# Set-up of a four-layer model: who splits the output weights and copies the first queries

## The chip, the cores and the metric

One core of one Trainium2 chip runs the whole program. The time is the device time of one execution in microseconds.

## The reference

The model adds four layers to x (2 batches, 1024 rows, 256 columns):

```python
x = x + attention0(x)   # layer norm, 16 heads of 64, one shared key/value head, queries and keys
                        # l2-normalised, causal, relative-position bias from a small MLP, null key
x = x + attention1(x)   # layer norm, scaled queries, bias read from memory, null key
x = x + moe2(x)         # 8 experts, two taken per row, and a shared expert
x = x + moe3(x)
# attention0, cut to what matters
sim  = concat([q . null_key, q @ k.T]) * 8 + concat([null_bias, bias])
attn = softmax(where(causal & mask, sim, -big))
out  = ln((attn @ concat([null_value, v])) @ Wout, g_out)
```

The change touches only the set-up for attention0. Weights are used as two float16 halves: high = f16(256 w), low = f16(256 w - high), and a product is three matrix products of halves.

## The kernel before, in words

Five engines (TensorE, VectorE, ScalarE, GpSimd, and SyncE for loads) each run a list written out in program order and meet at semaphores. The attention of both layers is one loop over head-steps n: a step T is a tile of 128 rows (16 steps over two layers), with 8 units u (four groups of four heads, two batches) of 4 heads, so 512 head-steps. The loop begins at n = -20: what stands at n < 0 is the set-up and the lead of the pipeline. With m, k = divmod(n, 4), an engine's work for unit u is written at fixed places: at k = 1 the query product of unit m + 3 (TensorE) and its squares and copy (ScalarE, L862, L864); at k = 2 the reciprocal root and scaling on GpSimd (L611 to L615); at k = 3 the transposes of unit m + 2 (TensorE L1679), the high half `q_b` (ScalarE L853), the low half into the lower partitions of `q_a` (VectorE L1285), and a copy of the high half into the upper partitions of `q_a` (GpSimd, `query_copy`, L558). Scores of head i come at n = i - 3 (L1655, L1656), `biased` and `neg_max` at n = i - 2 on VectorE (L1253), the exponential at i - 1, and transposes, halves (ScalarE L932, VectorE L1351) and the product with v from n = i.

Weights land in `stage` (two buffers). In the set-up ScalarE scales and rounds to the high half (`weight_half`, and `out_half` with two instructions L772 and L775 for each half of the output weights), and GpSimd makes the low half in pieces of 256 columns (`low_half`, L529): 2 pieces of wkv, 8 of wq, 8 of wo. It does the first wq pieces at n = -12 and the other six at n = -9; the wo pieces stand one at the end of each head-step from n = -7 to 0. The semaphore `job_done` counts all pieces; TensorE waits on it before it uses wq and wo, SyncE before it fills a stage buffer again.

The null key enters as 16 extra columns, `w_nk`: VectorE multiplies the rows of Wq with the null key (`null_product`, L1153), sums over each head (L1158) and splits the sums into halves (`null_columns`, L1140, L1141). TensorE multiplies with them at n = -7. The null logits of unit u are then two small GpSimd steps (L653, L654) at k = 3, m = u - 2; the first of unit 0 at n = -5.

The bias of attention0 comes from a table that the MLP fills in four rounds; the first (`table_scale`, `table_active2`, `table_out`, L1027, L1034, L1056) lies in the set-up, its rows go to memory and come back as `bias`.

Of the kernel before, what the change touches and what calls it, by code (L numbers as in the profile page):

```python
# [24 lines left out]
ALU = mybir.AluOpType  # L25
ACT = mybir.ActivationFunctionType
AX = mybir.AxisListType.X
# [66 lines left out]
def model(nc, a, out):  # L94
# [3 lines left out]
    with ctx:  # L98
# [324 lines left out]
        def round_at(n, at_):  # L423

            return n // STEP_N + 1 if n % STEP_N == at_ and 0 <= n < 3 * STEP_N else 0
# [63 lines left out]
        def _(pool):  # L489
# [35 lines left out]

            def low_half(n):
                jn, hi, lo, at_, w, gain, gc = pieces[n]
                pool.wait_ge(setup["half"], (2, 4 if at_ % INNER < UW else 6, 7 + at_ // 1024)[jn])
                gp.tensor_tensor(lo, stage[:, jn % 2, at_:at_ + w], hi, ALU.subtract).then_inc(job_done, 1)  # L529

            def piece(n):
# [23 lines left out]
            def query_copy(u):  # L555
# [2 lines left out]
                gp.tensor_copy(q_a[0:DH, u % 2, :], q_b[0:DH, u % 2, :]).then_inc(s["q_dup"], 1)  # L558
                pool.wait_ge(s["q_dup"], u + 1)

            def low_to(n):
                while split[0] < n:
                    low_half(split[0])
                    split[0] += 1

            pool.wait_ge(setup["mhalf"], 1)
            for n in range(FIRST, LAST):
# [13 lines left out]
                if n == -12:  # L581
                    pool.wait_ge(setup["nss"], 1)
                    link(gp.tensor_tensor(null_r[:, :], null_r[:, :], mhalf[:, 0:1], ALU.pow))
                    gp.tensor_scalar(null_r[:, :], null_r[:, :], 1e12, 1.0, ALU.min, ALU.mult)\
                        .then_inc(setup["nrinv"], 1)
                    low_to(job_end[0] + KC)
                    row_rstd(0)
                if round_at(n, ROOT_AT):
                    row_rstd(round_at(n, ROOT_AT))
                if k == 1 and 1 <= m <= NU:  # L590

                    u = m - 1
                    pool.wait_ge(s["o_raw"], u + 1)
                    pool.wait_ge(s["r_den"], u + 1)
                    if u >= 1:
                        pool.wait_ge(s["ot"], u)
                    last = gp.tensor_tensor(o_n[:, :, :], o_raw[:, :, :],  # L597
                                            r_den[:, :].unsqueeze(2).to_broadcast([P, HU, DH]), ALU.mult)
                    if halves_first(u):
                        link(last)  # L600
                        o_f = o_n[:, :, :].rearrange("p h d -> p (h d)")
                        link(gp.tensor_copy(o_16[:, 0, :], o_f))
                        last = gp.tensor_tensor(o_16[:, 1, :], o_f, o_16[:, 0, :], ALU.subtract)
                    last.then_inc(s["o_n"], 1)
                if k == 2 and 0 <= m + 3 < U0:

                    u = m + 3
                    pool.wait_ge(s["q_ss"], u + 1)
                    if u >= 1:
                        pool.wait_ge(s["q_nd"], u)  # L610
                    link(gp.tensor_tensor(q_r2[:, u % 2, :], q_ss[:, :], mhalf[:, 0:HU], ALU.pow))  # L611
                    link(gp.tensor_scalar(q_r2[:, u % 2, :], q_r2[:, u % 2, :], 1e12 / WS, 1.0, ALU.min, ALU.mult))
                    pool.wait_ge(s["q_na"], u + 1)
                    q_h = q_n[:, u % 2, :].rearrange("p (h d) -> p h d", h=HU)
                    gp.tensor_tensor(q_h, q_h, q_r2[:, u % 2, :].unsqueeze(2).to_broadcast([P, HU, DH]), ALU.mult)\  # L615
                        .then_inc(s["q_nd"], 1)
                g, at_g = divmod(n + 4, 2 * HU)
                if at_g == 0 and TILES * HG <= g < STEPS * HG:
# [3 lines left out]
                    blk = bias[:, g % 2, :, t * P:(t + 1) * P]  # L622
                    gp.affine_select(out=blk, in_=blk, compare_op=ALU.is_ge, fill=NEG, base=0,
                                     pattern=[[0, HU], [-1, P]], channel_multiplier=1).then_inc(s["bias"], 1)
                if k == 3 and -2 <= m < 0:
                    pool.wait_ge(s["q_nd"], m + 4)
                    pool.wait_ge(job_done, split[0])
                    query_copy(m + 2)
                if k == 3 and 0 <= m < NU:

                    u = m
# [10 lines left out]
                    if u >= 1:  # L642
# [1 line left out]
                    gp.tensor_tensor(o_null[:, :, :], null_v[:, :].unsqueeze(1).to_broadcast([P, HU, DH]),  # L644
                                     p_null[:, :].unsqueeze(2).to_broadcast([P, HU, DH]), ALU.mult)\
                        .then_inc(s["o_null"], 1)
                if k == 3 and 0 <= m + 2 < U0:

                    u = m + 2
                    T, at_ = divmod(u, UNITS)  # L650
                    hs = slice(at_ // B * HU, (at_ // B + 1) * HU)
                    pool.wait_ge(s["null_t"], T + 1)
                    link(gp.tensor_tensor(null_of(u), null_t[:, T % 2, at_ % B, hs], q_r2[:, u % 2, :], ALU.mult))  # L653
                    gp.tensor_tensor(null_of(u), null_of(u), null_b[0][:, hs], ALU.subtract).then_inc(s["null"], 1)  # L654
                for T in range(STEPS):
                    n0 = T * STEP_N
                    if n == n0 - 17:
# [40 lines left out]
                        gp.tensor_tensor(x_t, x_t, y_t, ALU.add).then_inc(s["x_new"], 1)  # L698
                if n == -9:
                    low_to(job_end[1])  # L700
                if n >= -7 and split[0] < job_end[2]:
                    low_to(split[0] + 1)
                if k == 1 and job_end[2] <= split[0] < job_end[9]\
                        and n >= max(2 * STEP_N, 2 * HU * load_at(pieces[split[0]][0])):

# [17 lines left out]
        def _(act):  # L723
# [44 lines left out]
            def out_half(c):  # L768

                act.wait_ge(s_stage[0], stage_value[2])  # L770
                src = stage[:, 0, c * 1024:(c + 1) * 1024]
                ac.activation(src, src, ACT.Copy, scale=WS).then_inc(act_chain, 1)  # L772
                halves[0] += 1
                act.wait_ge(act_chain, halves[0])
                ac.activation(flat(wo[0][:, 0])[:, c * 1024:(c + 1) * 1024], src, ACT.Copy).then_inc(setup["half"], 1)  # L775

            act.wait_ge(setup["vec"], 1)
            for kc in range(KC):
# [25 lines left out]
            for n in range(FIRST, LAST):  # L804
# [8 lines left out]
                            weight_half(1, kc, INNER, c0, c1)  # L813
                if n == -9:
                    table_tanh2(0, sc[0][:, 0:512])
                if n == -8:
                    out_half(0)
                    out_half(1)
                first, second = banks(n)
                i = n + 1  # L820
# [35 lines left out]
                if k == 1 and 0 <= m + 3 < NU:  # L856
                    u = m + 3
                    act.wait_ge(s["q_proj"], u + 1)
                    if u < U0:
                        if u >= 1:  # L860
                            act.wait_ge(s["q_ss"], u)
                        ac.activation(q_sq[:, :, :].rearrange("p h d -> p (h d)"), first[:, 0:UW], ACT.Square)\  # L862
                            .then_inc(s["q_sq"], 1)
                    ac.activation(q_n[:, u % 2, :], first[:, 0:UW], ACT.Copy, scale=1.0 if u < U0 else DH ** -0.5 / WS)\  # L864
                        .then_inc(s["q_na"], 1)

                def small():

# [94 lines left out]
        def _(dve):  # L963
# [173 lines left out]

            def null_columns(l):

                link(ve.tensor_copy(w_nk[l][:, 0, :, :], w_nkf[:, :, :]))  # L1140
                ve.tensor_tensor(w_nk[l][:, 1, :, :], w_nkf[:, :, :], w_nk[l][:, 0, :, :], ALU.subtract)\  # L1141
                    .then_inc(s["wnk"], 1)

            def null_product(kc):

                dve.wait_ge(setup["half"], 5 + kc)
                if kc == 0:
                    dve.wait_ge(setup["nrinv"], 1)
                    link(ve.scalar_tensor_tensor(null_kd[:, :], null_k[:, :], null_r[:, 0:1], k_scale[:, :],
                                                 ALU.mult, ALU.mult))  # L1150
                src = stage[:, 1, kc * INNER:(kc + 1) * INNER].rearrange("p (h d) -> p h d", h=H)
                prod = null_p.rearrange("p (h d) -> p h d", h=H)
                link(ve.tensor_tensor(prod, src, null_kd[:, :].unsqueeze(1).to_broadcast([P, H, DH]), ALU.mult))  # L1153

            def null_sum(kc):

# [47 lines left out]
            for n in range(FIRST, LAST):  # L1204
# [12 lines left out]
                if n == -10:  # L1217
                    table_active2(0, sc[0][:, 0:512])
                if n == -8:
                    null_product(1)  # L1220
                    table_out(0, sc[1][0:H, 0:2 * P])
                    null_sum(1)
                    null_columns(0)
                first, second = banks(n)
                if k == 1 and 1 <= m <= NU:
                    u = m - 1
# [54 lines left out]
                if k == 3 and 0 <= m + 2 < NU:  # L1281
                    u = m + 2
                    dve.wait_ge(s["q_hi"], 2 * (u + 1))
                    for e in range(2):
                        ve.tensor_tensor(heads(q_a[DH:P, u % 2, :], e),  # L1285
                                         first[e * DH:(e + 1) * DH, 0:UW].rearrange("p (c q) -> p c q", q=P),
                                         heads(q_b[0:DH, u % 2, :], e), ALU.subtract).then_inc(s["q_lo"], 1)
                def small():

                    for T in range(STEPS):  # L1290
# [74 lines left out]
                if n == N + 2:  # L1365
# [3 lines left out]
                    gate_weights(0)  # L1369
                    leaky(1)  # L1370
                    product(1)
                if (k == 1 and 0 <= m + 3 < U0 and n != -3) or n == -2:
                    u = m + 3
                    dve.wait_ge(s["q_sq"], u + 1)
                    if u >= 1:
                        dve.wait_ge(s["q_nd"], u)
                    ve.reduce_sum(q_ss[:, :], q_sq[:, :, :], AX).then_inc(s["q_ss"], 1)
                if n == -17:
                    row_gains(tp[1])
                    table_vectors()  # L1380
# [448 lines left out]
```

## Time and profile before

| | us |
|---|---|
| median of 3 runs | 1618.56 (1616.38 to 1621.02) |
| profiled execution | 1616.94, its span 1615.1 |
| TensorE busy | 1434.6 (89%) |
| VectorE busy | 1398.2 (87%) |
| ScalarE busy | 1168.1 (72%) |
| GpSimd busy | 903.7 (56%) |
| mean granted TensorE clock | 0.98 |

The names in the views are PE for TensorE, PEld for its weight loads, DVE for VectorE, ACT for ScalarE, POOL for GpSimd, SPq for SyncE's queue of transfers. Busy time is a sum over the instructions of an engine. An idle time in brackets is that of the engine just before the instruction, with what ended it. A row of the order of time merges neighbouring instructions of one line (x6 is six of them, the time that of all).

### The profile page before, as it was taken

Reading aid. Unit: us, or ns where it says so; the run is one execution under the profiler, and the core shown is the slowest. Engines: PE = TensorE matmul, PEld = TensorE weight load, DVE = VectorE, ACT = ScalarE, POOL = GpSimd, SP = SyncE. Lnnn points to the kernel's source line nnn. Section 1 sums busy time; section 2 is a strip of 40 time slices with the busy share of each in tenths; the row PEclk is TensorE's granted clock in tenths of the full one; section 3 lists DMA queues with packets and bytes.
Section 4 is the critical chain, followed back from the end, with each engine's and each line's share of the span. In section 5 each row is a group of like instructions: output and inputs, shape, how many; then the busy total and the mean of one; then the engine's idle time right before and its main releaser. Section 6 shows DMA issues by size and latency. Waiting matters only on the chain.

```text
span 1615.1 us, 45627 instructions
## 1 busy us (share of the span) xinstructions
PE 1434.6 (89%) x15680; PEld 1069.2 (66%) x15680; DVE 1398.2 (87%) x3629; ACT 1168.1 (72%) x3093; POOL 903.7 (56%) x1766
## 2 busy tenths in 40 slices
PE   4677778888999999977788999999999989999998
PEld 2455556666777777855666777777878756666665
DVE  6667888899999999977789998999999889888887
ACT  4566778888989999967788898989999633333332
POOL 6666778776756556577665344444343366632222
PEclk8789999999999999999999999999999999999999
DMA  6002211112222134012122122212223000000000
GB/s 158 18 28 69 71 48 54 60 67 73 80 87 93 48 107 131 9 47 67 54 61 79 60 75 87 84 68 88 100 106 106 2 27 20 1 1 1 14 14 27
DMA packets 49954, 96.50 MB, mean 60 GB/s; under 512 B 2922, under 2 KB 26560, under 8 KB 49728
## 3 DMA queue, kind: packets, MB, share of 16 engines
q1 hardware_dynamic: 48420, 92.93, 17.7%
q8 instruction: 129, 2.11, 0.5%
q10 hardware_dynamic: 1308, 0.67, 0.2%
q14 instruction: 97, 0.79, 0.2%
HBM read 91.41 MB, written 2.17 MB: 58 GB/s over the span
## 4 chain that ended last, share of the span: by engine, by line
PE 57%; DVE 20%; ACT 7%; issue 7%; POOL 4%; DVEq 0%; ACTq 0%; POOLq 0%
PE tp L1787 10%; DVE biased L1253 6%; PE sc L1655 6%; DVE p_lo L1351 5%; PE sc L1445 4%; PE sc L1447 4%; PE sc L1446 4%; PE sc L1656 4%; DVE q_a L1285 3%; PE aux L1445 3%; PE op L1445 3%; PE aux L1447 2%; PE aux L1446 2%; PE op L1447 2%; PE op L1446 2%
## 5 line engine op out<-in xcount | busy, mean ns | idle before, releaser
L1351 DVE TENSOR_TENSOR p_lo<-tp,p_hi 128x256 f16<-128x256 f32 (+3 forms) x896 | 424.8, 496 | 78.8 <-ACT p_hi L932 70.0
L1787 PE MATMUL tp<-ident,probs 128*128 128x128 f32 x2304 | 414.7, 280 | 24.6 <-DVE p_lo L1351 20.3
L932 ACT ACTIVATE p_hi<-tp 128x256 f16<-128x256 f32 (+3 forms) x896 | 385.2, 445 | 39.4 <-PE tp L1787 26.3
L832 ACT ACTIVATE probs<-biased,neg_max 128x256 f32<-128x256 f32 (+7 forms) x512 | 396.2, 774 | 14.7 <-DVE neg_max L1253 12.9
L1445 PE MATMUL op<-v_s,p_hi 128*128 128x64 f16 x2304 | 297.6, 194 | 28.2 <-DVE p_lo L1351 18.9
L1655 PE MATMUL sc<-k_a,q_a 128*128 128x512 f16 (+3 forms) x768 | 254.1, 331 | 65.9 <-DVE neg_max L1253 50.7
L1787 PEld LDWEIGHTS tp<-ident,probs 128*128 128x128 f32 x2304 | 261.6, 142 | 67.5 <-issue 29.0
L1446 PE MATMUL op<-v_s,p_hi 128*128 128x64 f16 x2304 | 297.2, 193 | 0.0
L1447 PE MATMUL op<-v_s,p_lo 128*128 128x64 f16 x2304 | 297.2, 193 | 0.0
L1445 PEld LDWEIGHTS op<-v_s,p_hi 128*128 128x128 f16 x2304 | 219.7, 99 | 47.7 <-DVE p_lo L1351 30.8
L1656 PE MATMUL sc<-k_b,q_b 128*128 128x512 f16 (+3 forms) x768 | 242.0, 329 | 0.0
L1446 PEld LDWEIGHTS op<-v_s,p_hi 128*128 128x128 f16 x2304 | 211.4, 98 | 9.7
L1447 PEld LDWEIGHTS op<-v_s,p_lo 128*128 128x128 f16 x2304 | 211.8, 98 | 0.0
L1253 DVE CUSTOM_DVE_ANT_0 biased<-sc,bias,neg_null 128x128 f32<-128x128 f32 (+7 forms) x256 | 205.7, 804 | 4.5 <-PE sc L1656 3.2
L1253 DVE CUSTOM_DVE_ANT_0 biased<-sc,bias,null_t 128x128 f32<-128x128 f32 (+7 forms) x256 | 205.8, 804 | 1.0
L552 POOL TENSOR_TENSOR p_lo<-probs,p_hi 128x512 f16<-128x512 f32 x80 | 92.6, 1158 | 175.1 <-ACT p_hi L802 175.1
L558 POOL COPY q_a<-q_b 64x512 f16<-64x512 f16 x128 | 77.6, 606 | 152.0 <-ACT q_b L853 148.9
L1655 PEld LDWEIGHTS sc<-k_a,q_a 128*128 128x128 f16 x768 | 74.9, 98 | 131.2 <-DVE neg_max L1253 73.2
L597 POOL TENSOR_TENSOR o_n<-o_raw,r_den 128x256 f32<-128x256 f32 x128 | 78.7, 615 | 138.6 <-DVE o_raw L1229 137.9
L802 ACT ACTIVATE p_hi<-probs 128x512 f16<-128x512 f32 x80 | 50.4, 630 | 130.8 <-DVE probs L1135 130.8
L1285 DVE TENSOR_TENSOR q_a<-aux,q_b 64x256 f16<-64x256 f32 x256 | 108.3, 423 | 24.9 <-ACT q_b L853 17.3
L796 ACT ACTIVATE biased<-sc 128x512 f32<-128x512 f32 x80 | 47.7, 596 | 89.6 <-PE sc L1447 89.6
(354 smaller groups left out, 3617.9 us busy)
## 6 DMA issues: line engine op xcount, KB each, us to landing
bias<-rel_table SPq DMA_DIRECT2D x4, 2048.0 KB, 9.1
bias<-in_fside_16xSxS SPq DMA_DIRECT2D x4, 2048.0 KB, 8.1
bias<-rel_table SPq DMA_DIRECT2D x4, 1792.0 KB, 7.3
bias<-in_fside_16xSxS SPq DMA_DIRECT2D x4, 1792.0 KB, 7.3
bias<-rel_table SPq DMA_DIRECT2D x4, 1536.0 KB, 6.2
bias<-in_fside_16xSxS SPq DMA_DIRECT2D x4, 1536.0 KB, 6.5
bias<-rel_table SPq DMA_DIRECT2D x4, 1280.0 KB, 5.6
bias<-in_fside_16xSxS SPq DMA_DIRECT2D x4, 1280.0 KB, 6.5
```

The source lines that it names most:

```text
L552: gp.tensor_tensor(h_lo[:, en % 4, :], h_f[:, en % 2, :], h_hi[:, en % 4, :], ALU.subtract)\
L832: ac.activation(probs[:, i % 2, 0:w], biased[:, i % 2, 0:w], ACT.Exp, bias=neg_max[:, u % 2, i % HU:i % HU + 1], scale=-1.0, accum_out=row ...
L932: ac.activation(p_hi[:, gi % 4, 0:nb * P], tp[gi % 2][:, 0:nb * P], ACT.Copy)\
L1253: ve.tensor_tensor_reduce(out=biased[:, i % 2, 0:w], in0=sc[i % 2][:, 0:w], in1=bias[:, g % 2, i % HU, 0:w], scale=-1.0, scalar=null_of(u) ...
L1285: ve.tensor_tensor(heads(q_a[DH:P, u % 2, :], e), first[e * DH:(e + 1) * DH, 0:UW].rearrange("p (c q) -> p c q", q=P), heads(q_b[0:DH, u % ...
L1351: ve.tensor_tensor(p_lo[:, gi % 4, 0:nb * P], tp[gi % 2][:, 0:nb * P], p_hi[:, gi % 4, 0:nb * P], ALU.subtract).then_inc(s["p_lo"], 1)
L1445: te.matmul(out_, l_hi, r_hi, start=first, stop=False)
L1446: te.matmul(out_, l_hi, r_lo, start=False, stop=False)
L1447: return te.matmul(out_, l_lo, r_hi, start=False, stop=last)
L1655: te.matmul(o_, q_a[:, u % 2, cols], k_a[layer][:, bt, c0:c0 + cw], start=True, stop=False)
L1656: last = te.matmul(o_, q_b[:, u % 2, cols], k_b[layer][:, bt, c0:c0 + cw], start=False, stop=True)
L1787: last = te.transpose(tp[gi % 2][:, jj * P:(jj + 1) * P], probs[:, n % 2, (j0 + jj) * P:(j0 + jj + 1) * P], ident[:, :])
```

## The change

In program order: the low pieces of wq at n = -12 on GpSimd are six instead of two, the other two stay at n = -9. The eight wo pieces leave GpSimd for VectorE, one at the end of each head-step from n = -1 to 6, and each is now one fused step from the unscaled weights. ScalarE's `out_half` is one instruction instead of two, and its two calls stand at n = -7 behind the queries' copy, and at the head of n = -4. The copies of the high half of units 0 and 1 go from GpSimd to VectorE, behind the low half. The null logits of unit 0 go from n = -5 to n = -6, ahead of the scaling of unit 1. On VectorE the second null product is cut in two with `table_out` between, the null columns use `scalar_tensor_tensor`, and the sum of squares of unit 1 goes from n = -7 to the end of n = -8.

```diff
@@ GpSimd
-                pool.wait_ge(setup["half"], (2, 4 if at_ % INNER < UW else 6, 7 + at_ // 1024)[jn])
+                pool.wait_ge(setup["half"], (2, 4 if at_ % INNER < UW else 6)[jn])
...
                     low_to(job_end[0] + KC)
                     row_rstd(0)
+                    low_to(job_end[0] + 3 * KC)
...
+                if n == -6:
+                    null_logits(0)
...
-                if k == 3 and -2 <= m < 0:
-                    pool.wait_ge(s["q_nd"], m + 4)
-                    pool.wait_ge(job_done, split[0])
-                    query_copy(m + 2)
...
-                if k == 3 and 0 <= m + 2 < U0:
...
+                if k == 3 and 1 <= m + 2 < U0:
+                    null_logits(m + 2)
...
-                if n >= -7 and split[0] < job_end[2]:
-                    low_to(split[0] + 1)
+                if n == 2 * STEP_N:
+                    pool.wait_ge(job_done, job_end[2])
+                    split[0] = job_end[2]
@@ ScalarE
-                ac.activation(src, src, ACT.Copy, scale=WS).then_inc(act_chain, 1)
-                halves[0] += 1
-                act.wait_ge(act_chain, halves[0])
-                ac.activation(flat(wo[0][:, 0])[:, c * 1024:(c + 1) * 1024], src, ACT.Copy).then_inc(setup["half"], 1)
+                ac.activation(flat(wo[0][:, 0])[:, c * 1024:(c + 1) * 1024], src, ACT.Copy, scale=WS)\
+                    .then_inc(setup["half"], 1)
...
-                if n == -8:
-                    out_half(0)
+                if n == -4:
                     out_half(1)
...
+                if n == -7:
+                    out_half(0)
@@ VectorE
-                link(ve.tensor_copy(w_nk[l][:, 0, :, :], w_nkf[:, :, :]))
-                ve.tensor_tensor(w_nk[l][:, 1, :, :], w_nkf[:, :, :], w_nk[l][:, 0, :, :], ALU.subtract)\
+                w_f = w_nkf[:, :, :]
+                link(ve.scalar_tensor_tensor(w_nk[l][:, 0, :, :], w_f, 1.0, w_f, ALU.mult, ALU.max))
+                ve.scalar_tensor_tensor(w_nk[l][:, 1, :, :], w_f, 1.0, w_nk[l][:, 0, :, :], ALU.mult, ALU.subtract)\
                     .then_inc(s["wnk"], 1)
...
+            def queries_sum(u):
+
+                dve.wait_ge(s["q_sq"], u + 1)
+                if u >= 1:
+                    dve.wait_ge(s["q_nd"], u)
+                ve.reduce_sum(q_ss[:, :], q_sq[:, :, :], AX).then_inc(s["q_ss"], 1)
+
+            def out_low(p_):
+
+                _, hi, lo, at_, w, _, _ = pieces[p_]
+                dve.wait_ge(setup["half"], 7 + at_ // 1024)
+                if p_ == job_end[1]:
+                    dve.wait_ge(job_done, job_end[1])
+                ve.scalar_tensor_tensor(lo, stage[:, 0, at_:at_ + w], WS, hi, ALU.mult, ALU.subtract).then_inc(job_done, 1)
...
                 if n == -8:
-                    null_product(1)
+                    null_product(1, 0, H // 2)
                     table_out(0, sc[1][0:H, 0:2 * P])
+                    null_product(1, H // 2, H)
                     null_sum(1)
                     null_columns(0)
+                    queries_sum(1)
...
+                    if u < 2:
+                        ve.tensor_copy(q_a[0:DH, u, :], q_b[0:DH, u, :]).then_inc(s["q_dup"], 1)
...
+                if (k == 1 and 0 <= m + 3 < U0 and n not in (-7, -3)) or n == -2:
+                    queries_sum(m + 3)
+                if -1 <= n < 7:
+                    out_low(job_end[1] + n + 1)
```

## Rows read from the trace of the kernel before

**Rows 1.** The page, part 1: busy us, share of the span, instructions.
```profile
PE 1434.6 (89%) x15680; PEld 1069.2 (66%) x15680; DVE 1398.2 (87%) x3629; ACT 1168.1 (72%) x3093; POOL 903.7 (56%) x1766
```

**Rows 2.** By stretch: us, busy of PE, PEld, DVE, ACT, POOL, clock, DMA, GB/s.
```profile
24.50:29.30 4.80, 2.60 (x20) 2.18 (x19) 4.66 (x9) 2.30 (x11) 1.53 (x4) 1.00 0.93 297
33.80:39.90 6.10, 1.16 (x15) 0.70 (x16) 1.69 (x5) 1.85 (x6) 5.65 (x11) 0.50 0.31 86
...
80.00:90.00 10.00, 6.46 (x35) 4.08 (x32) 5.07 (x16) 5.54 (x20) 4.49 (x10) 0.50 0.01 2
```

**Rows 3.** TensorE in order of time: start, us, line, idle before and releaser.
```profile
29.29 1.04 PE L1473 MATMUL sc<-moe_w 128*16 128x256 f32 x4 [2.20 <-DVE moe_w L1034]
...
34.67 0.69 PE L1679 MATMUL aux<-ident,q_n 128*128 128x128 f32 x2 [0.40 <-ACT q_n L864]
39.89 0.27 PE L1655 MATMUL sc<-k_a,q_a 128*128 128x128 f16 x1 [4.54 <-POOL q_a L558]
...
46.22 0.29 PE L1655 MATMUL sc<-k_a,q_a 128*128 128x128 f16 x1 [2.81 <-POOL q_a L558]
...
50.13 0.29 PE L1655 MATMUL sc<-k_a,q_a 128*128 128x128 f16 x1 [0.65 <-DVE neg_max L1253]
```

**Rows 4.** GpSimd in order of time, 23 to 40 us.
```profile
23.78 0.72 POOL L524 TENSOR_TENSOR r_rs<-r_rs,mhalf 128x2 f32<-128x2 f32 x1
27.38 0.70 POOL L665 TENSOR_TENSOR k_r<-k_ss,mhalf 128x2 f32<-128x2 f32 x1 [2.88 <-ACT v_s L898]
...
29.83 1.02 POOL L612 TENSOR_SCALAR q_r<-q_r 128x4 f32<-128x4 f32 x1
...
31.74 3.81 POOL L529 TENSOR_TENSOR wq<-stage,wq 128x256 f16<-128x256 f32 x6
...
37.25 0.23 POOL L612 TENSOR_SCALAR q_r<-q_r 128x4 f32<-128x4 f32 x1
...
38.93 0.60 POOL L558 COPY q_a<-q_b 64x512 f16<-64x512 f16 x1
```

**Rows 5.** ScalarE in order of time, 29 to 37 us.
```profile
29.89 1.06 ACT L772 ACTIVATE stage<-stage 128x1024 f32<-128x1024 f32 x1 [1.86 <-DMA stage<-in_L_cond_Wout]
...
33.98 0.37 ACT L862 ACTIVATE q_sq<-aux 128x256 f32<-128x256 f32 x1
...
35.40 0.78 ACT L853 ACTIVATE q_b<-aux 64x256 f16<-64x256 f32 x2 [0.50 <-PE aux L1679]
```

**Rows 6.** VectorE in order of time, 24 to 49 us.
```profile
24.54 0.73 DVE L1027 TENSOR_SCALAR moe_w<-moe_w,r_mv,r_rs 128x256 f32<-128x256 f32 x2 [1.29 <-POOL r_rs L524]
...
29.54 1.22 DVE L1153 TENSOR_TENSOR moe_w<-stage,null_kd 128x1024 f32<-128x1024 f32 x1
...
32.42 0.65 DVE L1140 CAST w_nk<-w_nkf 128x32 f16<-128x32 f32 x1
33.11 0.60 DVE L1141 TENSOR_TENSOR w_nk<-w_nkf,w_nk 128x32 f16<-128x32 f32 x1
...
36.21 0.88 DVE L1285 TENSOR_TENSOR q_a<-aux,q_b 64x256 f16<-64x256 f32 x2 [0.45 <-ACT q_b L853]
...
43.84 0.88 DVE L1285 TENSOR_TENSOR q_a<-aux,q_b 64x256 f16<-64x256 f32 x2 [1.15 <-ACT q_b L853]
...
48.80 0.29 DVE L1351 TENSOR_TENSOR p_lo<-tp,p_hi 128x128 f16<-128x128 f32 x1 [2.83 <-ACT p_hi L932]
```

**Rows 7.** One line or tile, or groups (busy, mean ns): prices, bias loads.
```profile
L1042 DVE TENSOR_SCALAR moe_w<-moe_w,g_c x2: 221/988/1756, 19.4 to 21.1; 128x16 f32<-128x16 f32 x2
...
L992 DVE TENSOR_TENSOR moe_w<-moe_w 128x512 f32<-128x512 f32 x1 | 0.7, 685 | 0.0
...
L1000 DVE SCALAR_TENSOR_TENSOR moe_w<-moe_w,rel_f 128x256 f32<-128x256 f32 x6 | 2.8, 478 | 0.0
...
L403 SPq DMA_DIRECT2D bias<-rel_table x2: 367/438/508, 32.9 to 33.3; - x2
...
DMA to landing us min/median/max: 3.4/3.5/3.7
```

More of the change, by code:

```diff
@@ L559, in query_copy, with null_logits @@
                 pool.wait_ge(s["q_dup"], u + 1)
+            def null_logits(u):
+                T, at_ = divmod(u, UNITS)
+                hs = slice(at_ // B * HU, (at_ // B + 1) * HU)
+                pool.wait_ge(s["null_t"], T + 1)
+                link(gp.tensor_tensor(null_of(u), null_t[:, T % 2, at_ % B, hs], q_r2[:, u % 2, :], ALU.mult))
+                gp.tensor_tensor(null_of(u), null_of(u), null_b[0][:, hs], ALU.subtract).then_inc(s["null"], 1)
             def low_to(n):
@@ L646, in _ @@
                         .then_inc(s["o_null"], 1)
-                if k == 3 and 0 <= m + 2 < U0:
[L649 to L654, printed above, removed]
+                if k == 3 and 1 <= m + 2 < U0:
+                    null_logits(m + 2)
                 for T in range(STEPS):
@@ L1138, in null_columns, with null_product @@
             def null_columns(l):
-                link(ve.tensor_copy(w_nk[l][:, 0, :, :], w_nkf[:, :, :]))
-                ve.tensor_tensor(w_nk[l][:, 1, :, :], w_nkf[:, :, :], w_nk[l][:, 0, :, :], ALU.subtract)\
+                w_f = w_nkf[:, :, :]
+                link(ve.scalar_tensor_tensor(w_nk[l][:, 0, :, :], w_f, 1.0, w_f, ALU.mult, ALU.max))
+                ve.scalar_tensor_tensor(w_nk[l][:, 1, :, :], w_f, 1.0, w_nk[l][:, 0, :, :], ALU.mult, ALU.subtract)\
                     .then_inc(s["wnk"], 1)
-            def null_product(kc):
+            def queries_sum(u):
[9 more added lines that the diff above has]
+                ve.scalar_tensor_tensor(lo, stage[:, 0, at_:at_ + w], WS, hi, ALU.mult, ALU.subtract).then_inc(job_done, 1)
+            def null_product(kc, h0=0, h1=H):
                 dve.wait_ge(setup["half"], 5 + kc)
-                if kc == 0:
+                if kc == 0 and h0 == 0:
                     dve.wait_ge(setup["nrinv"], 1)
@@ L1152, in null_product @@
                 prod = null_p.rearrange("p (h d) -> p h d", h=H)
-                link(ve.tensor_tensor(prod, src, null_kd[:, :].unsqueeze(1).to_broadcast([P, H, DH]), ALU.mult))
+                link(ve.tensor_tensor(prod[:, h0:h1], src[:, h0:h1],
+                                      null_kd[:, :].unsqueeze(1).to_broadcast([P, h1 - h0, DH]), ALU.mult))
             def null_sum(kc):
@@ L1371, in _ @@
                     product(1)
[L1372 to L1377, printed above, removed]
+                if (k == 1 and 0 <= m + 3 < U0 and n not in (-7, -3)) or n == -2:
+                    queries_sum(m + 3)
+                if -1 <= n < 7:
+                    out_low(job_end[1] + n + 1)
                 if n == -17:
```

## The prediction

> **What bounds the kernel now.** I read the page first. Over the whole span TensorE and VectorE are both nearly full (89% and 87%) [rows 1], but the change touches nothing after the first seven head-steps, so it can only move when the steady loop starts. I therefore went to the busy time by stretch, then to each engine's order of time from 20 to 60 us, and last to single lines and tiles that look dearer here than elsewhere. Three stretches matter [rows 2]. From 24.5 to 29.3 VectorE is busy 4.66 of 4.8 us while GpSimd is busy 1.53. From 33.8 to 39.9 TensorE does 1.16 us of work in 6.1, GpSimd 5.65: here the first scores wait for GpSimd. The row of 80 to 90 shows TensorE at the lower of its two levels (0.50, 1.2 GHz) after a stretch with gaps.
>
> In TensorE's order of time the transposes of the first queries start at 34.67, after a wait for ScalarE, the first scores at 39.89 after 4.54 idle, released by GpSimd's copy of the queries, and the fifth (first of the second unit) at 46.22 after 2.81 idle for the second copy [rows 3]. GpSimd's own list says why it is late: r_rs ends at 24.50, 2.88 us idle, then k_r at 27.38; six weight pieces of 0.635 us (3.81 for six) stand between 31.74 and 35.55, and pieces of the output weights stand before the first copy at 38.93 [rows 4]. ScalarE starts the output weights' four steps at 29.89 and reaches the second unit's squares only at 33.98; the first queries' high half follows at 35.40 [rows 5]. VectorE is dense up to 33.71 and then mostly waits [rows 6].
>
> **The change, part by part.** All durations are of the profiled execution: 1616.94 us, 1.84 around its span of 1615.10, and 1.62 under the median 1618.56 of the runs shown. The sum is made against 1616.94 and then set on the median.
>
> *ScalarE.* Two of the four steps of 1.06 us go, one stands behind the queries' squares, one behind the first unit's high half. Before, that block ran from 29.89 to 33.98 and held back squares whose product, six matmuls right behind the table's 1.04 us (to 30.33, [rows 3]), I estimate over at 31.7. Now the squares come at about 31.8, one step of 1.06 ends at about 33.5, and ScalarE is free when the null-column products end. So the query transposes no longer wait for it. The second step (about 1.1 us) lies in ScalarE's idle time before the first scores [rows 2, 5].
>
> *VectorE up to the null columns.* Call W the end of the null columns, 33.71 before (33.11 + 0.60). The two instructions took 0.65 and 0.60 beside GpSimd's pieces [rows 6]; a 16-column operation of the same kind took 0.22 when alone and 1.76 when GpSimd was in its mask step [rows 7]. I take 0.22 each: -0.81. That price stands if GpSimd is at nothing that collides; else the old one, so 0 to -0.81. The product in two halves costs 0.69 each instead of 1.22 [rows 6, 7]: +0.15. The table's output then waits for TensorE's 1.04 us (29.29 to 30.33) instead of lying behind the product: +0.15; it comes some 0.4 earlier itself, which the bias loads don't need: they were issued at 32.9 and 33.3 and landed 3.4 to 3.7 later, so by 37.0, and biased work starts after 38 in every case below [rows 7]. Without collisions W = 33.71 - 0.81 + 0.30 = 33.2.
>
> *Four weight pieces moved to 24.5.* They fill GpSimd's 2.88 us gap (4 x 0.635 = 2.54) [rows 4], and that looks free. It isn't certain. The rows show that the two engines block each other: GpSimd's tiny q_r step, 0.23 at 37.25, took 1.02 at 29.83, ending with VectorE's product of 29.54 to 30.77 [rows 4, 6]; VectorE's two null-column steps each ended just behind a piece of GpSimd. In 24.5 to 26.7 VectorE has four operations of those kinds: two scalings of 0.365 from 24.54, a small one, and the first product, twin of the 1.22 one [rows 6]. Each can find a piece in front of it (at most 4 x 0.63 = 2.5), or slip between two as the cast did (0). VectorE has no idle time from there to W, so what it loses goes into W, and with the product in front of k_r GpSimd loses a little too, which stays hidden behind W. I take the middle, 1.3: W = 34.5.
> The Trainium skill speaks against this edit: "SBUF — State Buffer", section "Who interferes with whom", says that a VectorE instruction with two inputs from SBUF contends with a GpSimd instruction that reads SBUF, whichever comes second being held for the other's whole length. By that the collision is near its full price and the fused form of the null columns, which still has two SBUF inputs, gives no protection by itself; by the rows' cast, which slipped between two pieces, it is less. With the full price the forecast would be 1.2 us worse.
>
> *From W to the first scores.* Products 0.4 behind W, transposes 0.7, high half 0.8, low half 0.9 (36.21 to 37.09) [rows 3, 5, 6], then VectorE's own copy of 64x512 f16. No row has it. Below it stands the 0.22 of a tiny operation, above it 0.69 of 512 columns [rows 7]; behind GpSimd's 1.02 us step it could wait up to as much again. I take 0.35. With the hand-overs the first scores are at W + 3.4 = 37.9, against 39.89: a gain of 2.0, or 3.3 without collisions, 0.8 with all of them. The moved null logits (two steps of 0.2) and the earlier q_ss stay under this.
> The skill's "VectorE: DVE Perf Modes", section "The TRN2 errata — SBUF-src ops pay a fixed extra latency per instruction", gives a fixed term of about 150 cycles and four 16-bit elements per cycle for a copy; as an estimate that is (150 + 512/4)/0.96 GHz = 0.29 us, which would change the sum by 0.06.
>
> *From there to the fifth scores.* Before 6.33 us (39.89 to 46.22), the end set by GpSimd's copy. That copy goes to VectorE at 4.8 us after the first scores (low half done; before at 43.84 + 0.88 = 44.72 [rows 6]), but in front of the third biased block now stand the copy (0.35) and the first output-weight piece, 128x256 by a fused step, 0.47 [rows 7]. The fifth scores need that block (0.43): 4.85 + 0.35 + 0.47 + 0.43 + 0.05 = 6.15. Gain 0.2 only: the wait on GpSimd becomes a wait on VectorE.
>
> *The eight pieces.* On GpSimd 8 x 0.64 = 5.1 us go; past the first copy they only filled waits. On VectorE they add 8 x 0.47 = 3.8 us, one per head-step. Those that come where VectorE waits cost nothing (2.83 idle before 48.80 [rows 6]); those directly ahead of a biased block that TensorE waits for cost all: at 50.13 it had waited 0.65 for that block [rows 3]. By the pattern of a unit (four head-steps) I count three of the seven others exposed: 3 x 0.47 = 1.4. Bounds 0 and 3.3.
>
> Sum: -2.0 - 0.2 + 1.4 = -0.8 us. That makes the profiled execution 1616.1 and the median 1618.56 - 0.8 = 1617.8.
>
> **Rivals.**
> (a) No collision, pieces hidden. For it: the cast slipped in, VectorE idle 2.8 us at 48.80. -3.3 - 0.2 = -3.5: 1615.1.
> (b) The clock follows. In 30 to 57 and again in 80 to 90 us TensorE runs at the lower level, each time after gaps. If the shorter start also keeps the level up in one of these, half of the 6.46 us busy there, 3.2, comes on top of (a)'s 3.5 (a gap of 4.5 us gone is what speaks for it; that the level fell by 33.8, ahead of the long gap, against): about -6.5, 1612.1.
> (c) Slower: VectorE becomes the bound of the first two units. Place: head-steps -1 to 6; price 3.8 us with all eight pieces exposed, against 2.2 won by the first scores and the copy. It decides from the fifth exposed piece on; all exposed gives 2.2 - 3.8: +1.6, 1620.2; with the full collision +2.8, 1621.4. Against it: the idle 2.83.
> (d) It does nothing: some 2 us are won at 40 us and wholly taken back by the first unit's pace. 1618.6.
>
> **How the numbers follow.** Forecast 0.42, (d) 0.18, (a) 0.20, (b) 0.10, (c) 0.10. A difference under 0.3% (4.9 us) can't be told from none here. Only (b) passes it on the fast side, and a part of (a) with a lucky level: 0.15. On the slow side it takes (c) and a clock stretch added (+3.2): 0.06. The rest, 0.79, is within. Range: from -6 of (b), cut to what leaves under 2 in 10 outside, to (c) with 1 us for the spread of a median: 1613.0 to 1621.5.
>
> **What would show it.** Right: first scores near 38 us, released by VectorE, null columns at about 0.2 each; GpSimd's pieces at 24.5 and VectorE's product or scalings near them longer than 1.23 and 0.37; TensorE waiting for neg_max at the fifth scores. A product at 1.23 with a start at 36.5 means (a); a lower-level stretch missing or added before 100 us means (b) or its opposite; TensorE's waits for neg_max up by 3 us between 40 and 62 means (c). First scores still at 39 or later would make my sum wrong.

## The result, and the profile after

The changed kernel takes 1621.11 us (median of 20 runs, 1619.25 to 1623.15), the kernel before 1617.35 (20 runs beside them, 1615.99 to 1621.14): ratio 1.002, 95% interval 1.0014 to 1.0025. It is 3.8 us slower, where 0.8 faster was forecast. The time lies inside the stated range, on the other side of "before" than the forecast. The forecast stood on a median of three runs, 1618.56, which is 1.2 above that of the twenty. And the prediction held that a difference under 4.9 us can't be told from none: with 20 runs of each kernel, 3.8 us stand clear of none. The profiled execution has a span of 1619.2 against 1615.1 us.

VectorE of the changed kernel in order of time (start, us, line, idle before and releaser), the lines that answer to [rows 6]:

```profile
9.49 0.75 DVE L1290 BATCH_NORM_STATS2 st<-x 128x6 f32<-128x256 f32 x2 [1.24 <-DMA x<-in_x]
...
25.22 1.43 DVE L1028 TENSOR_SCALAR moe_w<-moe_w,r_mv,r_rs 128x256 f32<-128x256 f32 x2 [1.29 <-POOL r_rs L524]
26.57 0.69 DVE L1166 SCALAR_TENSOR_TENSOR null_kd<-null_k,null_r,k_scale 128x64 f32<-128x64 f32 x1
27.30 1.60 DVE L1170 TENSOR_TENSOR moe_w<-stage,null_kd 128x1024 f32<-128x1024 f32 x1
...
33.45 0.47 DVE L1057 TENSOR_SCALAR moe_w<-sc,b_sb 16x256 f32<-16x256 f32 x1 [1.06 <-PE sc L1493]
...
35.87 0.19 DVE L1142 SCALAR_TENSOR_TENSOR w_nk<-w_nkf 128x32 f16<-128x32 f32 x1
36.10 0.19 DVE L1143 SCALAR_TENSOR_TENSOR w_nk<-w_nkf,w_nk 128x32 f16<-128x32 f32 x1
...
38.84 0.28 DVE L1309 COPY q_a<-q_b 64x512 f16<-64x512 f16 x1
...
44.57 0.41 DVE L1159 SCALAR_TENSOR_TENSOR wo<-stage,wo 128x256 f16<-128x256 f32 x1
45.01 0.35 DVE L1273 CUSTOM_DVE_ANT_0 biased<-sc,bias,neg_null 128x128 f32<-128x128 f32 x1
...
52.62 0.71 DVE L1159 SCALAR_TENSOR_TENSOR wo<-stage,wo 128x256 f16<-128x256 f32 x1
53.26 0.34 DVE L1273 CUSTOM_DVE_ANT_0 biased<-sc,bias,neg_null 128x128 f32<-128x128 f32 x1
```

The first row is the start of the work on x: it stands 0.68 us later than before (8.81), because that execution's load of x landed later. I take 0.68 off below; among the other profiled runs this offset lies between 0.09 and 0.74, and whether any of it belongs to the change is open. Then the reader sees four things. The scalings at 25.22 took 1.43 instead of 0.73, the small step 0.69 instead of 0.28, the product 1.60 instead of 1.23: the collisions. The table's output waited 1.06 us. The null columns and the copy of the queries are as cheap as costed (0.19 each, 0.28). And the output-weight pieces stand ahead of a `biased`: four of the eight directly (44.57, 49.80, 52.62 with 0.71 us, 56.83), the other four with one or two short steps between.

GpSimd of the changed kernel in order of time, against [rows 4]:

```profile
25.16 2.65 POOL L529 TENSOR_TENSOR wq<-stage,wq 128x256 f16<-128x256 f32 x4
28.06 1.39 POOL L666 TENSOR_TENSOR k_r<-k_ss,mhalf 128x2 f32<-128x2 f32 x1 [0.25 <-ACT v_s L899]
```

The four pieces lie beside VectorE's scalings, small step and product, and GpSimd lost time too: this `k_r` step took 1.39 us instead of 0.70.

TensorE of the changed kernel in order of time, against [rows 3]:

```profile
31.45 1.89 PE L1493 MATMUL sc<-moe_w 128*16 128x256 f32 x4 [3.71 <-DVE moe_w L1035]
...
39.51 0.26 PE L1675 MATMUL sc<-k_a,q_a 128*128 128x128 f16 x1 [2.43 <-DVE q_a L1309]
...
45.51 0.27 PE L1675 MATMUL sc<-k_a,q_a 128*128 128x128 f16 x1 [2.49 <-DVE neg_max L1273]
...
49.74 0.29 PE L1675 MATMUL sc<-k_a,q_a 128*128 128x128 f16 x1 [0.98 <-DVE neg_max L1273]
...
53.75 0.27 PE L1675 MATMUL sc<-k_a,q_a 128*128 128x128 f16 x1 [0.65 <-DVE neg_max L1273]
```

The first and fifth scores are released by VectorE now, as forecast, and both are earlier than before (39.89, 46.22). The loss comes after them. Busy time by stretch (us; PE, PEld, DVE, ACT, POOL; clock; DMA), kernel before:

```profile
37.00:57.00 20.00, 11.06 (x69) 7.79 (x70) 8.26 (x37) 9.05 (x36) 14.34 (x30) 0.50 0.06 17
57.00:65.00 8.00, 6.07 (x53) 4.67 (x52) 5.79 (x22) 5.45 (x21) 5.07 (x11) 0.97 0.04 11
```

and the changed kernel:

```profile
37.00:57.00 20.00, 10.89 (x69) 7.74 (x69) 12.07 (x46) 10.87 (x40) 9.68 (x21) 0.52 0.12 34
57.00:65.00 8.00, 6.47 (x30) 4.62 (x30) 4.47 (x15) 3.80 (x14) 4.33 (x9) 0.50 0.10 28
```

From 57 to 65 us TensorE is nearly all the time at the upper level before (0.97) and does 53 matmuls; in the changed kernel it is at the lower one (0.50), 6.47 us busy for 30. VectorE's busy time from 37 to 57 has gone from 8.26 to 12.07.

A table of one landmark per unit, the start of VectorE's sum of squares of the queries (read from the order of time, us), places the loss:

| sum of squares | before | changed | before_wo_dve | after_fill_units2 | after_slots |
|---|---|---|---|---|---|
| third | 42.00 | 41.61 | 41.48 | 41.96 | 41.92 |
| fourth | 49.00 | 48.27 | 48.27 | 47.88 | 47.52 |
| fifth | 56.27 | 56.50 | 56.51 | 56.03 | 54.78 |
| sixth | 63.95 | 67.07 | 66.48 | 64.47 | 62.47 |
| 21st | 190.44 | 194.16 | 193.73 | 189.86 | 189.70 |
| fourth to fifth | 7.27 | 8.23 | 8.24 | 8.15 | 7.26 |
| fifth to sixth | 7.68 | 10.57 | 9.97 | 8.44 | 7.69 |
| level up at, us | 57.6 | 65.0 | 64.3 | 56.9 | 56.7 |

Of the changed kernel's 4.1 us at the end (the spans), 3.7 are there at 190 us: 0.96 came between the fourth and the fifth sum and 2.89 between the fifth and the sixth. The recorded expectations below count these sums from zero: their "third to fourth" is the table's fourth to fifth. The last row gives the rise after which the level stays up until the dips that all have, from 73 us on. Shorter rises stand before it: 57.5 to 60.9 in before_wo_dve, 43.3 to 46.7 in both last columns, 50.1 to 53.5 in after_fill_units2. All these landmarks and levels are of one execution of each kernel; that the other executions have the same is not shown.

### The profile page after: what moved, and what is told of

Same layout as the page of the kernel before. It is cut to its first block, busy times and chain, and to the rows that moved or that the text cites. A ratio compares the mean times of both kernels' runs of the same rounds, so it can differ in the third digit from the quotient of the medians.

```text
span 1619.2 us, 45624 instructions
## 1 busy us (share of the span) xinstructions
PE 1438.3 (89%) x15680; PEld 1072.2 (66%) x15680; DVE 1403.1 (87%) x3640; ACT 1166.3 (72%) x3091; POOL 898.7 (56%) x1756
## 4 chain that ended last, share of the span: by engine, by line
PE 57%; DVE 20%; ACT 7%; issue 7%; POOL 4%; DVEq 0%; ACTq 0%; POOLq 0%
PE tp L1807 10%; DVE biased L1273 6%; PE sc L1675 6%; DVE p_lo L1373 5%; PE sc L1465 4%; PE sc L1467 4%; PE sc L1466 4%; PE sc L1676 4%; DVE q_a L1305 3%; PE aux L1465 3%; PE op L1465 3%; PE aux L1467 2%; PE aux L1466 2%; PE op L1467 2%; PE op L1466 2%
## 5 line engine op out<-in xcount | busy, mean ns | idle before, releaser
L1373 DVE TENSOR_TENSOR p_lo<-tp,p_hi 128x256 f16<-128x256 f32 (+3 forms) x896 | 424.6, 496 | 78.7 <-ACT p_hi L933 69.8
L1675 PE MATMUL sc<-k_a,q_a 128*128 128x512 f16 (+3 forms) x768 | 254.3, 331 | 65.2 <-DVE neg_max L1273 54.9
L606 POOL TENSOR_TENSOR o_n<-o_raw,r_den 128x256 f32<-128x256 f32 x128 | 78.7, 615 | 141.3 <-DVE o_raw L1249 139.0
```

The lines of the kernel that those rows point to most:

```text
L1373: ve.tensor_tensor(p_lo[:, gi % 4, 0:nb * P], tp[gi % 2][:, 0:nb * P], p_hi[:, gi % 4, 0:nb * P], ALU.subtract).then_inc(s["p_lo"], 1)
L1675: te.matmul(o_, q_a[:, u % 2, cols], k_a[layer][:, bt, c0:c0 + cw], start=True, stop=False)
```

## The experiments

Two theories. Clock: the kernel loses because TensorE's level rises at 65.0 us instead of 57.6. VectorE: it loses because the eight pieces stand in VectorE's queue ahead of `biased` (and the wq pieces collide). All comparisons are ratios to the kernel before on the same chip. "Filler" is a product of the identity with itself into a part of `op` that nothing reads.

**Fillers in the set-up's gaps, in both kernels.**

```diff
+            def filler(c):
+                pe.wait_ge(setup["lgh"], 1)
+                pe.wait_ge(setup["ident16"], 1)
+                for _ in range(c):
+                    te.matmul(op[:, 0:P], ident16[:, :], ident16[:, :], start=True, stop=True)
```

> The changed kernel with 70 products of ident16 with itself (128x128, about 0.107 us each at 1.2 GHz, results never read) in TensorE's idle gaps of the set-up: 24 before the table's product, 10 before the null columns, 18 before the first scores, 18 before the fifth. Clock theory (the changed kernel loses some 3 us because TensorE stays at the lower level until 65 us instead of 57): with the gaps filled the level rises sooner, the time falls by 2 to 4 us to 1617 to 1619 and the 2.9 us jump between the fourth and fifth unit is gone. VectorE theory (the eight output-weight pieces on VectorE and the port collisions cost the time): fillers change nothing, 1620.5 to 1622.

> The kernel before with 74 such fillers (14, 6, 34 and 20 at the same four places). Clock theory: a little faster than before, 0 to 3 us, if the level rises before 57 us; same as before if the windows of low level stay. VectorE theory: same as before, within 1 us.

Measured: after_fill 1620.57, ratio 1.001 (1.0001 to 1.0019); before_fill 1618.26, ratio 0.9995 (0.9987 to 1.0004). In after_fill the level rose at 61.3 and fifth to sixth took 9.86: the 2 to 4 us that the clock theory promised did not come. In before_fill the level was up at 55.6, fifth to sixth took 7.46, and the profiled run was 2.0 us ahead at 190 us; it lost 1.6 of it behind 1138 us, where the low stretch near 1300 us lasted 6.8 us instead of 3.4. Both effects are small beside their intervals: neither theory falls.

**One part of the changed kernel undone.**

```diff
# after_pieces_late
                     row_rstd(0)
-                    low_to(job_end[0] + 3 * KC)
# after_wo_pool: ScalarE's two steps again, and on GpSimd, not on VectorE
+                if n >= -1 and split[0] < job_end[2]:
+                    low_to(split[0] + 1)
...
-                if -1 <= n < 7:
-                    out_low(job_end[1] + n + 1)
```

> The changed kernel with the four wq pieces back at n = -9 on GpSimd. Both theories: null columns done about 1.5 to 2 us earlier than in the changed kernel, since VectorE's scalings and first product are not held. VectorE theory: the whole is faster by that, 1.5 us, to 1619.5. Clock theory: the time goes with where the low level ends, so either side of 1621, by up to 3 us, and not by what W gained.

> The changed kernel with the low half of the output weights on GpSimd again (at n = -1 to 6, one piece per head-step) and ScalarE's two steps for each high half. VectorE theory: VectorE loses 8 x 0.42 us of work, scores of the fifth head some 0.8 us earlier, the first three units 1 to 2 us shorter, 1619 to 1620. Clock theory: little by itself; a change above 2.5 us only together with a level that rises at another time.

Measured: after_pieces_late 1621.30, ratio 1.0015 (1.0006 to 1.0024); after_wo_pool 1618.04, ratio 0.9993 (0.9984 to 1.0002). The wq pieces had cost VectorE what was expected. VectorE of after_pieces_late in order of time:

```profile
25.29 0.74 DVE L1027 TENSOR_SCALAR moe_w<-moe_w,r_mv,r_rs 128x256 f32<-128x256 f32 x2 [1.28 <-POOL r_rs L524]
25.93 0.28 DVE L1165 SCALAR_TENSOR_TENSOR null_kd<-null_k,null_r,k_scale 128x64 f32<-128x64 f32 x1
26.25 1.22 DVE L1169 TENSOR_TENSOR moe_w<-stage,null_kd 128x1024 f32<-128x1024 f32 x1
...
33.59 0.19 DVE L1141 SCALAR_TENSOR_TENSOR w_nk<-w_nkf 128x32 f16<-128x32 f32 x1
33.82 0.58 DVE L1142 SCALAR_TENSOR_TENSOR w_nk<-w_nkf,w_nk 128x32 f16<-128x32 f32 x1
```

Scalings, small step and product are back at 0.74, 0.28 and 1.22, the null columns are done at 34.40 instead of 36.29, first scores at 37.87 instead of 39.51, and still the whole is not faster beyond the interval: fourth to fifth took 8.23 again and fifth to sixth 9.56, with low stretches up to 54.9 and from 58.3 to 61.7. Putting the output weights' pieces back on GpSimd gave 4.3 us against the changed kernel's 1.002; fourth to fifth was 7.27 again. That is more than the 1 to 2 us that the VectorE theory had promised; the level also rose earlier, at 61.8. Its fifth to sixth took 9.12 us and not before's 7.68, so with no piece on VectorE a part of the level's loss was still there in this execution.

**That part alone, in the kernel before.** GpSimd's eight pieces go, VectorE makes them at the end of head-steps -1 to 6 as `tensor_tensor(lo, stage, hi, subtract)`.

> The kernel before with one part of the change alone: the eight low pieces of the output weights on VectorE, one at the end of each head-step from -1 to 6, as a difference of stage and high half. VectorE theory: from the third to the fourth sum of squares 8.23 us instead of 7.27 (as in the three kernels that have the pieces on VectorE), some 1 us more in the unit after, 1 to 3 us slower than before in all, although GpSimd's first copies come earlier. Clock theory alone: no difference from the pieces themselves; only if the level rises later than 57 us, then 1.5 to 3.

Measured: 1621.65, ratio 1.0022 (1.0013 to 1.0031). This one edit costs all that the whole change costs. Its fourth and fifth sums of squares start at 48.27 and 56.51, the changed kernel's at 48.27 and 56.50; fifth to sixth took 9.97, with the level up at 57.5, down again at 60.9 and up at 64.3. Who waited for whom on TensorE from 39 to 65 us (us in total, times, longest), before_wo_dve:

```profile
PE sc L1666 <- DVE neg_max L1262: 4.3, 3, 2.6
PE sc L1666 <- POOL q_a L558: 3.8, 1, 3.8
```

and the kernel before:

```profile
PE sc L1655 <- POOL q_a L558: 7.3, 2, 4.5
PE sc L1655 <- DVE neg_max L1253: 0.6, 1, 0.6
```

The 4.3 are not all new. The longest, 2.6, stands at the fifth scores, where the kernel before waits 2.8 for GpSimd's second copy; it has other names, not more length. What the pieces add is in the other two waits, 1.7 instead of 0.6.

**Fillers inside the first two units of the changed kernel,** 31 of them, in gaps before products with v, the seventh scores and the table's turn. In the first form the helper's wait also stood ahead of every product with v of the whole loop:

```diff
             def filler(c):
+                if c == 0:          # only in after_fill_units2
+                    return
                 pe.wait_ge(setup["ident16"], 1)
                 for _ in range(c):
                     te.matmul(op[:, 2 * P:3 * P], ident16[:, :], ident16[:, :], start=True, stop=True)
...
+                filler({3: 7}.get(n, 0))                  # before the scores
...
+                        filler({2: 3, 4: 11, 6: 3}.get(n, 0))   # before the product with v
+                        filler(7 if n == 7 else 0)              # before the table's turn
```

> The changed kernel with 31 unread 128x128 products (0.107 us each at 1.2 GHz) in the gaps that TensorE has inside the first two units (3 before the second product with v, 7 before the seventh scores, 11, 3, and 7 before the table's turn). Clock theory: the level rises before 65 us (57 to 61), the stretch between the fourth and fifth sum of squares shrinks from 10.57 us by 1 to 2.5, the whole 1618.5 to 1620 where the changed kernel has 1621 to 1622. VectorE theory: no gain, or 0.5 us slower.

Measured: 1621.89, ratio 1.0025 (1.0013 to 1.0038, 7 runs). The level was up for good at 49.4, fourth to fifth took 7.53 and fifth to sixth 7.72 with all eight pieces in place, the kernel was 1.25 us ahead of before at 190 us, and 3.0 behind at 1138: 4 us went in small steps. The waits are the suspect, so it ran again without them.

> The in-unit fillers of after_fill_units in the changed kernel again, without the wait that stood ahead of every product with v in the whole loop (that kernel had gained 2.9 us between the fourth and the fifth unit and lost 4 us again from 260 to 1138 us in small steps). Clock theory: the stretch from fourth to fifth sum of squares stays near 7.7 us and the gain lasts: 2.5 to 4.5 us under the changed kernel, 1617 to 1618.5. VectorE theory (the pieces cost their time on VectorE whatever the level): at most 1 us better than the changed kernel, 1620 to 1621.

Measured: 1617.19, ratio 0.9995 (0.9987 to 1.0004). With nothing added but work that nobody reads, 4 us come back (1.002 to 0.9995), and the only difference from the first form is the wait, so the loss there was the wait's. Busy time by stretch, after_fill_units2:

```profile
37.00:57.00 20.00, 12.56 (x95) 8.88 (x94) 12.54 (x49) 11.08 (x40) 10.24 (x21) 0.67 0.14 38
57.00:65.00 8.00, 5.78 (x54) 4.47 (x55) 6.29 (x23) 5.32 (x20) 4.50 (x11) 1.00 0.06 16
```

TensorE is busier by 1.7 us up to 57, then at the upper level, with 54 matmuls where the changed kernel had 30. A part stays: fourth to fifth 8.15, fifth to sixth 8.44.

**The pieces on VectorE, but where it waits.**

```diff
+                if n == -2:                       # before the sum of squares
+                    for p_ in range(3):
+                        out_low(job_end[1] + p_)
+                if n == -1:                       # before the low half of the queries
+                    for p_ in range(3, 5): ...
+                if n == 1:                        # before the second p_lo
+                    for p_ in range(5, 8): ...
-                if -1 <= n < 7:
-                    out_low(job_end[1] + n + 1)
```

> The changed kernel with the eight VectorE pieces moved into stretches in which VectorE waits: three before the sum of squares at head-step -2, two before the low half at -1, three at 1 before the second p_lo. VectorE theory: the fourth to fifth scores and the third to fourth sum of squares go back to 7.27 us, 3 to 4 us under the changed kernel, 1617 to 1618.5. Clock theory: the time follows the level; better than the changed kernel only if the level rises before 65 us.

Measured: 1616.89, ratio 0.9994 (0.9985 to 1.0003). Fourth to fifth 7.26, fifth to sixth 7.69: the kernel before's own pace, with the same 8 instructions on the same engine. VectorE of after_slots in order of time, no piece ahead of a `biased` that TensorE waits for:

```profile
40.50 1.09 DVE L1159 SCALAR_TENSOR_TENSOR wo<-stage,wo 128x256 f16<-128x256 f32 x3
...
42.52 0.76 DVE L1159 SCALAR_TENSOR_TENSOR wo<-stage,wo 128x256 f16<-128x256 f32 x2
43.75 0.88 DVE L1311 TENSOR_TENSOR q_a<-aux,q_b 64x256 f16<-64x256 f32 x2 [0.48 <-ACT q_b L852]
...
46.12 1.09 DVE L1159 SCALAR_TENSOR_TENSOR wo<-stage,wo 128x256 f16<-128x256 f32 x3
```

Its level rose at 56.7, before the kernel before's 57.6, without a filler. The 1.4 us that it should keep from the earlier fifth scores don't show in the median: 0.9994 is not clear of 1.

**Combinations, for a version that beats both.** after_wo_pool and after_slots with the wq pieces late, each also with fillers in the set-up's gaps.

> The same with the four wq pieces at n = -9 again. Both: null columns done 0.7 to 2 us earlier than in after_slots, first scores about 37.5 to 38.5; 0 to 2 us faster than after_slots, by the level.

> The same with 54 unread products in TensorE's gaps of the set-up (12, 8, 20, 14). Candidate for the fastest: fifth scores before 43.5 us, 3 to 5 us under the kernel before, 1614 to 1616.

> The changed kernel without its two suspected costs: low pieces of the output weights on GpSimd (two ScalarE steps each half) and the four wq pieces at n = -9 again. If the two costs add: first scores at about 37.5 to 38, and 2 to 3 us faster than before by 60 us (1616 to 1617.5). If the clock decides: any time within 2 us of before's, with the level's stretches to explain it.

> The same with 58 fillers in TensorE's four gaps of the set-up (12, 8, 22, 16). Both theories: the fastest of all, first scores at 37.5 to 38 and the level up by 55 us: 3 to 5 us under the kernel before at 260 us, 1614 to 1616.5 in all.

| kernel | median us | ratio to before | interval |
|---|---|---|---|
| after_slots_late | 1616.12 | 0.9986 | 0.9976 to 0.9996 |
| after_slots_late_fill | 1616.53 | 0.9992 | 0.9983 to 1.0 |
| after_wo_pool_late | 1616.59 | 0.9986 | 0.9977 to 0.9995 |
| after_wo_pool_late_fill | 1615.87 | 0.998 | 0.997 to 0.9989 |

All are on the fast side (the second reaches 1.0); the last is 2.8 us under the 1618.70 of before beside it, the best here. None is clear of the others, and the fillers in the set-up's gaps moved the ratio by +0.0006 in one pair and -0.0006 in the other.

after_wo_pool_late was expected 2 to 3 us ahead of before by 60 us; its profiled execution was 1.0 behind at the sixth sum of squares (65.00 against 63.95). It has no piece on VectorE, its fourth to fifth took 7.26, and yet fifth to sixth took 10.50, with the level up only at 63.7. So the pieces are not the only thing that can keep the level down there. That execution, of 1619.39 us, is the slowest of its kernel's 11, with a median of 1616.59; that the others had the level up sooner would fit, and is not shown. after_wo_pool_late_fill was expected 3 to 5 us ahead at 260 us and was 1.1 ahead.

The expectations of the other two were half right: after_slots_late_fill was 3.1 us ahead at 546 us and 3.2 at 1138, but its span is only 1.5 under before's, the rest went after that; after_slots_late has its first scores at 38.18, as expected. Runs of one kernel spread over 3.5 to 6 us here.

## Why the prediction was wrong, step by step

**The failed step is the eight pieces.** The text counted three of seven others exposed, 1.4 us, and left the clock out of this term; in the profiled execution it is 3.8 us (0.96 and 2.89). By their waits the pieces cost 0.96 from the fourth to the fifth sum (8.23 against 7.27, the level low all through in both) and 0.76 from the fifth to the sixth (8.44 in after_fill_units2 against 7.68, the level up at 56.9 and 57.6): 1.7, so the exposed count was nearly right. What was missing is what comes on top through TensorE's level: 10.57 instead of 8.44 for fifth to sixth, 2.1 us, with the level up at 65.0 instead of 56.9. The split is rough: in after_fill_units, with the level up from 49.4 on, the two stretches took 7.53 and 7.72, and the pieces cost less. The prediction had the level's mechanism as a bonus in rival (b) and, on the slow side, as a stretch of 3.2 us added to (c) at 0.06; it never let it follow from the pieces. That the pieces cause the loss is shown by adding them alone (before_wo_dve), by taking them away (after_wo_pool) and by moving them (after_slots); that much of it goes through the level, by fillers with the pieces in place (after_fill_units2). Why the level rises when it does stays open: after_wo_pool_late shows it late without them.

**Rival (c)** had the place right (head-steps -1 to 6). That its time nearly fits (1621.4 with full collision, measured 1621.11) is luck: it was 2.8 us above a base that was 1.2 too high, measured are 3.8, and not all eight pieces were exposed, but about four of them and the level came on top.

**Collisions at 24.5.** Taken at 1.3 of 0 to 2.5. The first product ends at 28.90 - 0.68 = 28.22 instead of 26.73: 1.5, the middle was nearly right. But 0.9 came on top that was costed at 0.15: the table's output waited 1.06 us, because TensorE's four products took 1.89 at the lower level (0.50), not 1.04. So W was 36.29 - 0.68 = 35.6, not 34.5. This is the second term that was mis-sized. The rule of the Trainium skill cited in the prediction ("SBUF — State Buffer", "Who interferes with whom") agrees with the trace where it applies: the product and the small step, with two inputs in SBUF, took 1.60 and 0.69 instead of 1.23 and 0.28, and the fused form did not protect, 0.58 instead of 0.19 beside a piece in after_pieces_late. The two scalings (1.43 instead of 0.73) have one such input, apart from two values per row, and are not covered by the rule as cited. Its consequence for the time, 1.2 us worse, did not show: undoing the collisions gave a ratio of 1.0015 beside 1.002, inside each other's intervals.

**From W to the first scores.** Forecast 3.4, measured 39.51 - 36.29 = 3.22; the copy took 0.28 (0.35 taken; 0.29 estimated from the Trainium skill's "VectorE: DVE Perf Modes", section "The TRN2 errata — SBUF-src ops pay a fixed extra latency per instruction"). The first scores were 1.1 us earlier than before instead of 2.0, by W's error.

**To the fifth scores.** 6.00 us against 6.15 forecast, and TensorE waited for neg_max, as said. Net of the start 1.4 us were won here.

**Null columns** 0.19 each (0.22 taken), **ScalarE** free at its point, though the queries' squares came at 34.61 and not at 31.8, since TensorE's products before them were late; **bias loads** not in the way though much closer than said: issued at 35.5 and 35.9 in the changed kernel instead of 32.9 and 33.3, because the table was later.

In sum, against before and net of the start: -1.4 at the fifth scores, +1.7 for the pieces, +2.1 for the level, together 2.4 at the sixth sum of squares. At 190 us it is 3.0: the first dip of the level lasted 17.0 us (78.7 to 95.7) instead of 13.6 (78.0 to 91.6), and why is open.

## What to carry to other kernels

An engine that is idle more than half the time (VectorE, 8.26 us busy of 20) has no room at the end of each step if the next thing in its queue is what the bounding engine waits for; put such work in front of an instruction whose own wait is long, which cost nothing here for the same eight pieces. Where a short wait of TensorE falls into a stretch at its lower level, price also what a later rise would cost, and with both signs: here it was more than the wait itself. A gain at the first landmark of a pipeline says little; follow one landmark per unit until the difference stays.

## What the runs showed of the hardware

- A filler that nobody reads can pay: 31 unread products of 128x128 in TensorE's gaps inside the first two units turned a ratio of 1.002 into 0.9995. Fillers of 54 to 74 such products in the set-up's gaps moved it by -0.001 to +0.0006 in four pairs, none clear of noise.
- A wait that is long satisfied is not free in TensorE's queue: one ahead of every product with v and every head-step cost about 4 us between 190 and 1138 us (after_fill_units, from 1.25 ahead to 3.0 behind; without these waits, in after_fill_units2, from 0.6 ahead to 0.4, and the ratio was 0.9995 instead of 1.0025).
- The same four fp32 products of the table took 1.04 or 1.89 us, and the gap just ahead of them doesn't say which: 1.04 after 2.20 us idle in the kernel before, 1.89 after 3.71 in the changed kernel and 1.89 after 2.08 in before_wo_dve.
- The clock row of a profile is to be checked against the pace of the products. In before_wo_dve it says 1.00 up to 36.9 us, but the wq products of 256 columns between 24.2 and 32.7 us follow each other at 0.21 us, the pace that they have at 0.50 elsewhere (0.11 at 1.00). The same holds for 24 to 26 us of the kernel before, so the clock in the first row of [rows 2] is in doubt. From 39 to 70 us, pace and row agree in every profile here. TensorE of before_wo_dve in order of time:

```profile
24.55 0.42 PE L1458 MATMUL aux<-wq,moe_w 128*128 128x256 f16 x1
24.76 0.42 PE L1456 MATMUL aux<-wq,moe_w 128*128 128x256 f16 x1
...
29.82 1.89 PE L1484 MATMUL sc<-moe_w 128*16 128x256 f32 x4 [2.08 <-DVE moe_w L1035]
```

- A fused step with two inputs in SBUF took 0.55 to 0.59 instead of 0.19 us beside GpSimd's pieces (after_slots_late, after_pieces_late), where the plain cast before took 0.65.
